# Six row turns of one wave taken from TensorE to VectorE block transposes and transfers inside SBUF, and one load of norm rows moved ahead in a queue

## What is computed

```
attn_out = softmax(x Wq (x Wk)^T / 16) x Wv Wp + bp
cms_out  = gelu(attn_out cW1 + cb1) cW2 + cb2 + one_hot(code)
modifier = gelu([attn_out, cms_out] mW1 + mb1) mW2 + mb2
x = clip(x + cms_out + modifier, 0, 1)
for layer in 0, 1, 2:                       # the adapters
    h = gelu(x W_down[role] + b_down[role])         # 256 -> 128
    y = x + h W_up[role] + b_up[role]               # 128 -> 256
    x = layernorm(y) * gamma[role] + beta[role]
```

## Time and profile before

| | |
|---|---|
| median of 3 runs | 354.27 us (353.74 to 354.35) |
| the profiled execution, its own time | 353.92 us |
| its span, first to last instruction | 352.1 us |
| busy TensorE matmul / VectorE / ScalarE / GpSimd | 340.7 / 203.2 / 169.3 / 61.2 us |
| granted TensorE clock, mean | 1.000 of full speed |

### The profile page before, as it was taken

One profiled execution on the slowest core, in us unless ns is written; L12 is line 12 of the kernel. 1 busy time (PEld: TensorE's weight loads), 2 busy tenths in 40 slices (PEclk: granted clock), 3 DMA queues, 4 the chain that ended last, 5 costly groups with the idle time before them and its releaser, 6 DMA issues.

```text
span 352.1 us, 6686 instructions
## 1 busy us (share of the span) xinstructions
PE 340.7 (97%) x2259; PEld 283.5 (81%) x2259; DVE 203.2 (58%) x487; ACT 169.3 (48%) x337; POOL 61.2 (17%) x96
## 2 busy tenths in 40 slices
PE   6799999999999999999999999999999999999994
PEld 6686687788878888888877777877899999999962
DVE  6066367251353875466464665463689777454584
ACT  3465686464534544554254455353356454534421
POOL 2710140000040110001310110013221125100221
PEclk9999999999999999999999999999999999999999
DMA  6674799279110441200185997203867543298001
GB/s 215 187 237 149 183 124 145 26 165 164 32 60 0 118 120 31 96 30 15 54 279 154 264 290 238 61 32 99 207 151 207 146 128 84 70 290 329 20 0 45
DMA packets 32248, 46.14 MB, mean 131 GB/s; under 512 B 6396, under 2 KB 16950, under 8 KB 32214
## 3 DMA queue, kind: packets, MB, share of 16 engines
q1 hardware_dynamic: 30454, 41.72, 45.1%
q0 software_dynamic: 1392, 3.80, 3.7%
q10 hardware_dynamic: 368, 0.20, 0.2%
HBM read 43.60 MB, written 4.48 MB: 137 GB/s over the span
## 4 chain that ended last, share of the span: by engine, by line
PE 85%; DVE 5%; POOL 2%; ACT 2%; issue 2%; DMA 2%; SPq 0%; DVEq 0%; POOLq 0%
PE bank L331 12%; PE bank L333 12%; PE bank L332 12%; PE bank L1447 8%; PE bank L1452 8%; PE bank L1448 7%; PE bank L1491 4%; PE bank L1470 4%; PE bank L1351 2%; PE bank L1369 2%; PE bank L1309 2%; PE bank L1522 2%; DMA adapter_rows<-packed_rows 1%; PE bank L1570 1%; ACT h_full L811 1%
## 5 line engine op out<-in xcount | busy, mean ns | idle before, releaser
L811 ACT ACTIVATE h_full<-bank,bias 128x512 f32<-128x512 f32 (+1 forms) x80 | 48.2, 602 | 108.5 <-PE bank L333 103.0
L1043 DVE TENSOR_TENSOR h_lo<-h_full,h_hi 128x512 fp32r<-128x512 f32 (+1 forms) x80 | 46.7, 584 | 63.0 <-ACT h_hi L815 61.9
L731 POOL TENSOR_TENSOR rstd<-moments,minus_half 128x1 f32<-128x1 f32 x39 | 23.1, 591 | 169.6 <-DVE moments L1109 169.5
L815 ACT ACTIVATE h_hi<-h_full 128x512 fp32r<-128x512 f32 (+1 forms) x80 | 43.7, 546 | 2.5
L1101 DVE TENSOR_TENSOR window_y<-bank,window_x 128x256 f32<-128x256 f32 x39 | 16.5, 422 | 39.2 <-PE bank L1470 30.9
L1447 PE MATMUL bank<-h_hi,m_hi 128*128 128x512 f32 (+1 forms) x80 | 30.2, 387 | 0.2
L1447 PE MATMUL bank<-h_hi,c_hi 128*128 128x512 f32 (+1 forms) x80 | 30.2, 386 | 0.2
L331 PE MATMUL bank<-at_hi,c_hi 128*128 128x512 f32 (+1 forms) x80 | 29.3, 366 | 0.0
L331 PE MATMUL bank<-at_hi,m_hi 128*128 128x512 f32 (+1 forms) x80 | 29.1, 364 | 0.0
L333 PE MATMUL bank<-at_lo,c_hi 128*128 128x512 f32 (+1 forms) x80 | 27.8, 348 | 0.0
L333 PE MATMUL bank<-at_lo,m_hi 128*128 128x512 f32 (+1 forms) x80 | 27.8, 348 | 0.0
(11 more groups left out here) (237 smaller groups left out, 728.2 us busy)
## 6 DMA issues: line engine op xcount, KB each, us to landing
adapter_w<-packed_w SPq DMA_DIRECT2D x44, 256.5 KB, 3.5
adapter_rows<-packed_rows SPq DMA_DIRECT2D x36, 256.0 KB, 3.9
stage<-in_L_cond_mW SPq DMA_DIRECT2D x6, 512.0 KB, 4.5
mixed_w<-packed_w SPq DMA_DIRECT2D x8, 256.5 KB, 4.9
stage<-in_L_cond_cW SPq DMA_DIRECT2D x4, 512.0 KB, 5.8
last_w<-packed_w SPq DMA_DIRECT2D x2, 769.5 KB, 6.2
up_bias<-in_L_cond_b_up SPq DMA_DIRECT2D x12, 128.0 KB, 6.2
adapter_rows<-packed_rows SPq DMA_DIRECT2D x24, 64.0 KB, 2.2
```

Source lines behind the costliest of these rows:

```text
L731: pool.tensor_tensor(slot.rstd[:, :], slot.moments[:, 1:2], minus_half[:, :], ALU.pow)\
L811: act.activation(h_full[:, n % 2, rows], bank[n % 2][:, rows], ACT.Gelu, bias=bias[:, b:b + 1])\
L815: act.activation(h_hi[:, n % 2, rows], h_full[:, n % 2, rows], ACT.Copy).then_inc(h_hi_ready, 1)
L1043: dve.tensor_tensor(h_lo[:, n % 2, rows], h_full[:, n % 2, rows], h_hi[:, n % 2, rows].bitcast(F32), ALU.subtract).then_inc(h_lo_ready, 1)
```

## The change

`SPREAD` names six of the eight turns of the first wave: (2, 1), (3, 1) and (0, 2), (1, 2), (2, 2), (3, 2). For these:

- TensorE makes no transposes and ScalarE no copy.
- VectorE transposes slot.x in blocks of 32 by 32 into `block_rows` (two buffers), one instruction behind the norm and, where there is one, the residual sum L1101 of the same spot. It reads every fourth feature, so a run of 32 elements has a step of 16 bytes.
- SyncE's queue waits for that and issues four transfers of 32 KB each (one per quarter of the rows) from `block_rows` to `window_xT`, in pieces of 256 bytes. They put the blocks on all 128 partitions. `window_xT` has three buffers in place of two. In the queue the four stand behind the norm rows that follow the item's weights, ahead of the next item's weights.
- The down product waits for the transfers and reads its moving operand as four runs of 32 columns, 256 bytes apart.

Apart from that, the norm rows of item (3, 2) are loaded ahead of the role reads and weights of window 4, and not behind them. Six semaphores of the routing at the start are merged into others, with the same waits.

```
+SPREAD = [(w, 1) for w in WAVES[1][2:]] + [(w, 2) for w in WAVES[1]]
+RING = 3
...
         def turned(wave, spot):
-            return [(w, at // 4 + 1) for w, at in turns(wave, spot) if at % 4 == 3 and 1 <= at // 4 + 1 < LAYERS]
+            return [(w, at // 4 + 1) for w, at in turns(wave, spot)
+                    if at % 4 == 3 and 1 <= at // 4 + 1 < LAYERS and (w, at // 4 + 1) not in SPREAD]
+
+        def spread(wave, spot):
+            return [(w, layer + 1) for w, layer in norms(wave, spot) if (w, layer + 1) in SPREAD]
...
+        def blocks_of(n):
+            return window_xT[:, (n + 2) % RING, :, :].rearrange("p k m -> p (k m)").rearrange("p (q k r) -> p q k r", q=Q, k=VB)
...
+            def move_blocks(w, layer):
+
+                n = moves[w, layer]
+                sp.wait_ge(blocks_turned, n + 1)
+                if n + 2 >= RING:
+                    sp.wait_ge(filled[7], use["D", *last_in_place(n)] + 1)
+                for q in range(Q):
+                    sp.dma_start(blocks_of(n)[:, q, :, :].rearrange("p k r -> p (k r)"),
+                                 block_rows[quarter(q), n % 2, :].rearrange("p (f m) -> p f m", f=Q))\
+                        .then_inc(blocks_in[n % RING], 16)
...
             for n, w, layer in items:
+                if n and items[n - 1][1:] in moves:
+                    move_blocks(*items[n - 1][1:])
+                ahead = (w, layer) == (MIXED[0], 0)
+                if ahead:
+                    window_rows(*items[n - 1][1:])
                 window_weights(w, layer)
-                if 0 < n <= len(items) - len(ending):
+                if 0 < n <= len(items) - len(ending) and not ahead:
                     window_rows(*items[n - 1][1:])
...
+                for w, layer in spread(wave, spot):
+                    n = moves[w, layer]
+                    dve.wait_ge(slot_of(w).x_ready, item(w, layer - 1) + 1)
+                    if n >= 2:
+                        move_is_in(dve, n - 2)
+                    dve.transpose(block_rows[:, n % 2, :].rearrange("p (f k r) -> p k f r", f=Q, k=VB),
+                                  slot_of(w).x[:, :].rearrange("p (k i f) -> p k f i", f=Q, k=VB)).then_inc(blocks_turned, 1)
...
+                    elif (w, layer) in SPREAD:
+                        move_is_in(pe, moves[w, layer])
                     else:
                         pe.wait_ge(emptied[7], use["T", w, layer] + 1)
...
                     for vb in range(VB):
-                        rows = (xT[:, vb, columns(w)] if layer == 0
-                                else window_xT[:, order["T", w, layer] % 2, vb, :])
+                        rows = (xT[:, vb, columns(w)].rearrange("p (q r) -> p q r", q=Q) if layer == 0
+                                else blocks_of(moves[w, layer])[:, :, vb, :] if (w, layer) in SPREAD
+                                else window_xT[:, order["T", w, layer] % 2, vb, :].rearrange("p (q r) -> p q r", q=Q))
```

More of the change, by code:

```diff
@@ L168, in build @@
         slots = [Slot(n) for n in range(SLOTS)]
-        window_xT = sb("window_xT", [P, 2, VB, P])
+        window_xT = sb("window_xT", [P, RING, VB, P])
         window_h = sb("window_h", [P, 2, P])
+        block_rows = sb("block_rows", [P, 2, V])
         cms = sb("cms", [P, VB, GR])
@@ L266, in build @@
         onehot_ready = sem("onehot_ready")
-        code_ready = sem("code_ready")
         rows_turned = sem("rows_turned")
@@ L322, in build @@
         emptied = {b: sem(f"emptied{b}") for b in (2, 3, 5, 6, 7)}
+        blocks_turned = sem("blocks_turned")
+        blocks_in = [sem(f"blocks_in{n}") for n in range(RING)]
         first_w_in = sem("first_w_in")
@@ L413, in turned, with last_in_place, move_is_in @@
         def turned(wave, spot):
-            return [(w, at // 4 + 1) for w, at in turns(wave, spot) if at % 4 == 3 and 1 <= at // 4 + 1 < LAYERS]
+            return [(w, at // 4 + 1) for w, at in turns(wave, spot)
+                    if at % 4 == 3 and 1 <= at // 4 + 1 < LAYERS and (w, at // 4 + 1) not in SPREAD]
+        def spread(wave, spot):
+            return [(w, layer + 1) for w, layer in norms(wave, spot) if (w, layer + 1) in SPREAD]
+        moves = {}
+        for wave in WAVES:
+            for spot in range(SPOTS):
+                for move in spread(wave, spot):
+                    moves[move] = len(moves)
+        def last_in_place(n):
+            return ([(w, 1) for w in WAVES[1][:2]] + list(moves))[n + 2 - RING]
+        def blocks_of(n):
+            return window_xT[:, (n + 2) % RING, :, :].rearrange("p k m -> p (k m)").rearrange("p (q k r) -> p q k r", q=Q, k=VB)
+        def move_is_in(engine, n):
+            engine.wait_ge(blocks_in[n % RING], 16 * Q * (n // RING + 1))
         def bank_of(kind, w, layer=0):
@@ L925, in _ @@
             dve.wait_ge(id_consts, 3)
-            dve.tensor_scalar(earlier[:, :], batch_id[:, :], own_id[0:B, 0:1], None, ALU.is_gt).then_inc(earlier_ready, 1)
+            dve.tensor_scalar(earlier[:, :], batch_id[:, :], own_id[0:B, 0:1], None, ALU.is_gt).then_inc(pd_clear, 1)
             for a in (first_attention, second_attention):
@@ L950, in _ @@
             link(dve.tensor_copy(own_role_col[:, :], own_role))
-            dve.wait_ge(own_ready, 1)
-            dve.wait_ge(roles_counted, 1)
+            dve.wait_ge(role_row_ready, 2)
+            dve.wait_ge(roles_turned, 2)
             link(dve.tensor_copy(counts_i[:, :], totals))
@@ L1263, in _ @@
             pe.matmul(bank[4][0:B, 0:1], role_row[:, 1, :], ones[0:1, 0:1], start=True, stop=True).then_inc(roles_turned, 1)
-            pe.wait_ge(earlier_ready, 1)
-            pe.wait_ge(own_ready, 1)
+            pe.wait_ge(pd_clear, 1)
+            pe.wait_ge(role_row_ready, 2)
             pe.matmul(bank[5][0:B, 0:ROLES], ones[:, 0:B], own_onehot[:, :], start=True, stop=True)
             pe.matmul(bank[5][0:B, ROLES:2 * ROLES], earlier[:, :], own_onehot[:, :], start=True, stop=True)\
-                .then_inc(roles_counted, 1)
+                .then_inc(roles_turned, 1)
             turn_weights(0)
@@ L1487, in after @@
                             for q in range(WIN):
-                                ins = pe.matmul(bank[b][quarter(q), 0:KD], rows[:, quarter(q)], batch_w(w, layer, q)[:, down],
+                                ins = pe.matmul(bank[b][quarter(q), 0:KD], rows[:, q, :], batch_w(w, layer, q)[:, down],
                                                 start=(vb == 0), stop=(vb == VB - 1))
```

11 lines of the change are left out of this document (4 added, 7 removed).

## The result

The changed kernel takes 353.27 us (median of 22 runs, 352.82 to 354.73), the kernel before 354.32 (22 runs, 353.74 to 355.82): a ratio of 0.997, interval 0.996 to 0.998. Once more on another occasion it was 352.46 (12 runs) against 353.61 (30), 0.9969 [0.9957, 0.9982]. So the change gives 1.05 to 1.15 us, where the prediction had 1.36; the first interval alone spans 0.7 to 1.4.

The account below looks back on a forecast made before the run. TensorE was taken to bound the kernel, busy 17.00 of 17.00 us in the changed stretch. Pairs 0.96 and norm rows 0.40, all additions priced 0, made 1.36 us off the median 354.27: 352.9 us, range 352.2 to 353.8.

Parts of the forecast that it names:

- Turns (2, 1), (2, 2), (3, 2): Three transpose pairs removed from TensorE with nothing due behind them: 0.22 us each, 0.66 gained.
- Turn (3, 1): Pair removed ahead of D8 on TensorE, which waits for hidden block 8's high part anyway: gain 0.
- Turns (0, 2) and (1, 2): Two pairs (0.44 us) removed ahead of Z, which waits for VectorE: 0.30 us gained together.
- Block transpose: Six added on VectorE, 0.43 us each, hidden in idle stretches before the low parts at spots 7 and 8: price 0.
- the bound of 0.5: Block transpose length in us above which each excess was to delay Z through the low parts at spots 7 and 8.
- The moved norm rows: Item (3, 2)'s rows loaded earlier end VectorE's 0.52 us wait near 180.88 and TensorE's gap in group 2's D0: 0.40 gained.
- Transfers and the operand in four runs: 24 added transfers landing before their down products, and 6 down products reading 128-byte runs at unchanged speed: price 0.
- The median of before: Starting time of the sum, 354.27 us, as the profiled execution of 353.92 lay 0.35 below it.
- slow block transposes (0.9 us): Rival: strided read slows them, so pairs (0, 2) and (1, 2) give nothing; gain 1.06 us, 353.2; chance 0.20.

Follow-up runs that it names:

- e11_pfirst: Changed kernel with the second part of the softmax (row sums, pd transposes) ahead of the window's statistics at H11 on VectorE: 352.05 us beside 352.46 of the changed kernel.
- e10_twice: Changed kernel with each of the six block transposes made twice, one behind the other, same result: 353.07 us, ratio 0.9982 to the kernel before.
- e6_contig: Changed kernel with the block transpose reading 32 neighbouring features (step 4 bytes, not 16), so down products multiply wrong pairs: 353.19 us in one run.
- e1_rest: Changed kernel with no turn spread and the norm rows in their old place: 354.37 us, ratio 1.0012 to the kernel before.
- e3_turns: Changed kernel with the six turns spread but the norm rows in their old place: 353.64 us, ratio 0.9990 to the kernel before.
- e4_early: Changed kernel with each block transpose between the norm and the residual sum of its spot, not behind the sum: 353.05 us, ratio 0.9976 to the kernel before.
- e2_rows: Changed kernel with only the norm rows of item (3, 2) moved ahead, all turns by TensorE: 354.18 us, ratio 0.9999 to the kernel before.

## Why the prediction was right

The sum was 1.36 us and the measured gain 1.05 and 1.15: the time fell as forecast, and lies in the range, while the sum was 0.2 to 0.3 too large. By its steps:

- **Turns (2, 1), (2, 2), (3, 2), predicted 0.66.** Right, a little low: 0.22 for (2, 1), and 0.52 for the two behind Z (+.30 to -.22): 0.74. The Trainium skill, "TensorE: Matmul & The Clock Gate" (back-to-back issue gap), gives an estimate of 0.16 for each pair; here they are worth 0.22 to 0.26, so a row of this kernel was the better source.
- **Turn (3, 1), predicted 0.** Right. D8 waits for the high part and 0.25 us pass in place of the pair. The offset is +.59 on both sides of it.
- **Turns (0, 2) and (1, 2), predicted 0.30 together.** Right: 0.29 (+.59 to +.30). They give 0.52 up to 154.8, and 0.23 of it is lost again at Z, which waits for pd. That this wait is the limit, e11_pfirst and e10_twice show from both sides.
- **Block transpose, predicted 0.43 us, price 0.** The size was wrong, the price right. It takes 0.64: 0.435 for the transpose, as predicted from its neighbours, and 0.20 for the step of 16 bytes. The Trainium skill, "SBUF — State Buffer" (the note on cachelines), spoke against this read and was right in direction; the factor is 1.47, where I had estimated 2. It cost nothing because the room is 0.61 us at spot 7 and 0.71 at spot 8 from start to start (e6_contig), and the transpose takes 0.62 of it. I had read the room from the idle times, 0.53 and 0.54, and VectorE's instructions overlap by some 0.08 (147.33 to 147.94 is 0.61, while the idle time in rows 5 is 0.53). So the bound of 0.5 was 0.1 too low at spot 7, and the fit there is just so. That an excess reaches Z through softmax, table load, gelu and low part, as the prediction said, e10_twice shows: 0.65 us too much at spot 7, Z late by 0.61.
- **The moved norm rows, predicted 0.40: this step failed in its size.** Its mechanism is right: with the rows ahead no profile shows the wait. But the 0.40 was that of one execution, 0.41 in the table, and three others of the old order show 0.07, 0.26 and 0.27. The term should have been about 0.25. The times don't settle it: at full clock the rows alone give 0.1 against before and 0.3 against e1_rest, and e3_turns to e4_early is 0.68. But e4_early also has another order on VectorE, and its profile owes 0.25 of its lead to the end (-.69 to -.94, where e3_turns stays at -.38), which has nothing to do with the rows.
- **Transfers and the operand in four runs, predicted 0.** Right.
- **The median of before** as a start for the sum was right. The two profiled executions give 0.68 us, too little, for they had different starts and ends (the table's first and last columns).

1.03 for the turns and 0.25 for the rows is 1.28, and the runs give 1.05 to 1.15. The rest of 0.1 to 0.2 may be the merged semaphores and third buffer (e1_rest, which has only these, was 0.13 us slower than before, 0.2 at full clock, interval 0.9998 to 1.0026), or chance. It stays open. That the block transpose cost nothing was luck in part: its size was 0.2 us off, and at spot 7 it fits to within 0.01.

Of the rivals, slow block transposes (0.9 us) came nearest: they were slower than forecast, but 0.62 from start to start still fits.

## What to carry to other kernels

A wait that ends with a transfer is a term with a spread (0.17 to 0.52 us here): take a second profile of the same kernel before you put its length into a sum. Where work is hidden in an idle stretch, ask what waits behind it, on the same engine and on others that it feeds: at spots 4, 5, 6 and 9 a second transpose cost nothing, at spots 7 and 8 together 0.61 us, by VectorE's own order and by ScalarE's softmax at once. At spot 2 even one cost 0.5, and moving it behind one sum gave that back. When the engine that bounds the kernel gets faster, look at once for what it now waits for; here the softmax one place earlier gave 0.41 us, nearly as much as two pairs.

## What the hardware showed that I had not expected

The clock of TensorE can fall at the start of an execution. In the profile of e2_rows (355.16 us, mean clock 0.995) the offset at 21 us is +1.9, against +0.6 to +0.7 in the three other profiles of its set. Its windows of 1 us (busy time of TensorE, its weight loads, VectorE, ScalarE, GpSimd; then the granted clock, and the DMA engines' share and GB/s):

```profile
14.00:15.00 1.00, 0.03 (x1) 0.00 (x0) 0.32 (x2) 0.60 (x1) 0.94 (x1) 1.00 0.46 127
15.00:16.00 1.00, 0.37 (x2) 0.37 (x3) 0.00 (x0) 0.00 (x0) 0.70 (x2) 0.77 0.36 86
16.00:17.00 1.00, 1.00 (x6) 0.91 (x5) 0.00 (x0) 0.21 (x1) 0.69 (x2) 0.50 0.33 91
...
19.00:20.00 1.00, 1.00 (x6) 0.87 (x6) 0.00 (x0) 0.34 (x1) 0.00 (x0) 1.00 0.62 184
```

TensorE waited 1.60 us for its gathered rows, until 15.63, with 0.03 us of work between 14 and 15 us; from 15.5 to 19 us the clock was at 0.50 (the 1.2 GHz level), and the execution was 1.2 us behind the others of its set from there on. In the first profile of before the clock stayed at 1.00 here, and no microsecond from 10 to 17 has less than 0.28 us of work. No other kept profile has a clock below 1.00 ahead of 347 us. That the wait brought the fall about is not shown, nor how often it comes.

A second thing is GpSimd's instruction of one element per partition: the same one took 0.86 us in one execution and 0.57 in another of the same program, and 0.2 to 0.3 us of the kernel's time hung on it each time.
